# Taking 81 matmuls whose results nobody reads out of TensorE's instruction stream, at fifteen places

## What is computed

```python
x = x + L0_xattn(ln(x), ctx)   # 16 heads, causal mask: only the first 64 context rows of a batch count
x = x + L0_attn(ln(x))         # keys and values through a latent of width 64
x = x + L0_ffn(ln(x))          # bf16, 32 experts, top 4 by sigmoid gate, and a shared expert
x = x + L1_xattn(ln(x), ctx)   # one shared key/value head of width 16, all 1601 context rows
x = x + L1_attn(ln(x))         # causal attention, its own residual and layernorm with gamma, beta inside
x = x + L1_ffn(ln(x))          # 8 experts, each token goes to the one with the largest gate
```

## Time and profile before

| | |
|---|---|
| time, three runs | 552.41 us median (551.35 to 553.02) |
| the profiled execution | 552.53 us, span 550.6 us |
| busy share of the span | PE 94%, PE weight loads 66%, DVE 59%, ACT 55%, POOL 23% |
| matmuls | 6427, of which 81 by L1305 |
| mean granted TensorE clock | 0.996 |

### The profile page before, as it was taken

How to read it: one execution, slowest core, us unless ns; L and a number is a source line. 1 busy time by engine, 2 the same in 40 slices (tenths; PEclk the granted TensorE clock), 3 DMA queues, 4 the chain that set the end, 5 groups by cost and what they waited for, 6 DMA issues and landing times.

```text
span 550.6 us, 15198 instructions
## 1 busy us (share of the span) xinstructions
PE 519.7 (94%) x6427; PEld 363.7 (66%) x6427; DVE 325.7 (59%) x672; ACT 300.3 (55%) x511; POOL 124.2 (23%) x217
## 2 busy tenths in 40 slices
PE   3999999889999999889999999999979999999997
PEld 2666567546665666435776767676556657999996
DVE  4455475276666665768999999998146685011011
ACT  0356566676656565358887777877714412432221
POOL 5203602644333333340000000000060043000004
PEclk9999999999999999999999999999999998999999
DMA  8914620805554453820000000000080001798823
GB/s 325 402 45 162 228 92 9 284 8 149 146 158 138 147 155 99 301 83 2 4 3 4 4 2 4 3 4 4 2 307 1 1 2 39 240 353 271 309 90 95
DMA packets 35074, 64.37 MB, mean 117 GB/s; under 512 B 3296, under 2 KB 24800, under 8 KB 34624
## 3 DMA queue, kind: packets, MB, share of 16 engines
q1 hardware_dynamic: 34480, 62.35, 34.3%
q0 software_dynamic: 384, 1.05, 0.6%
q10 hardware_dynamic: 144, 0.01, 0.0%
HBM read 59.40 MB, written 4.00 MB: 115 GB/s over the span
## 4 chain that ended last, share of the span: by engine, by line
PE 84%; DVE 8%; POOL 2%; DMA 2%; ACT 2%; issue 2%; SPq 0%; POOLq 0%; DVEq 0%; ACTq 0%
PE ps L1342 14%; PE ps L1612 10%; PE ps L1743 9%; PE ps L1711 8%; PE ps L1757 7%; PE ps L1626 7%; PE ps L1935 6%; PE ps L1443 4%; PE ps L1317 2%; PE ps L1456 2%; PE ps L1469 2%; PE ps L1423 2%; DVE region L1119 1%; DMA ctx64T<-in_ctx64T 1%; PE ps L1367 1%
## 5 line engine op out<-in xcount | busy, mean ns | idle before, releaser
L1119 DVE TENSOR_REDUCE region<-ps 128x1 f32<-128x512 f32 x192 | 124.1, 687 | 17.9 <-PE ps L1711 17.9
L807 ACT ACTIVATE region<-ps 128x1024 f32<-128x1024 f32 (+1 forms) x112 | 105.9, 963 | 19.7 <-PE ps L1743 19.2
L1711 PE MATMUL ps<-ctx_kT,region 96*32 96x512 bf16 x768 | 82.0, 383 | 2.5 <-DVE region L1119 1.8
L1743 PE MATMUL ps<-region,ctx_kT 98*32 98x512 bf16 x832 | 72.5, 381 | 0.6 <-ACT region L785 0.4
L1757 PE MATMUL ps<-region,ctx_v 128*32 128x128 f32 (+1 forms) x1664 | 70.2, 272 | 0.0
L1612 PE MATMUL ps<-region 128*128 128x512 f16 x264 | 62.9, 379 | 0.3 <-DMA region<-in_moe 0.3
L1757 PEld LDWEIGHTS ps<-region,ctx_v 128*32 128x32 f32 (+1 forms) x1664 | 56.7, 109 | 9.4 <-issue 0.3
L857 ACT ACTIVATE region<-ps,ctx_v 128x128 f32<-128x128 f32 x88 | 25.2, 369 | 60.8 <-PE ps L1342 60.8
L502 POOL TENSOR_TENSOR region<-region 128x512 f32<-128x512 f32 x33 | 38.2, 1157 | 64.7 <-ACT region L734 63.3
L1626 PE MATMUL ps<-region 128*128 128x256 bf16 x384 | 47.2, 273 | 0.9 <-DVE region L1066 0.9
L1626 PEld LDWEIGHTS ps<-region 128*128 128x128 bf16 x384 | 37.4, 98 | 12.3 <-DVE region L1066 1.5
(11 more groups left out here) (230 smaller groups left out, 839.9 us busy)
## 6 DMA issues: line engine op xcount, KB each, us to landing
region<-in_w SPq DMA_DIRECT2D x15, 1024.0 KB, 8.5
region<-in_ctxT SPq DMA_DIRECT2D x8, 1601.0 KB, 7.9
region<-gates SPq DMA_DIRECT2D x30, 256.0 KB, 3.4
ctx_kT<-in_w SPq DMA_DIRECT2D x7, 1024.0 KB, 7.3
region<-in_moe SPq DMA_DIRECT2D x33, 192.0 KB, 2.4
attn_weights<-in_wall SPq DMA_DIRECT2D x1, 2152.0 KB, 21.9
slots_x<-zeros SPq DMA_DIRECT2D x1, 1408.0 KB, 10.5
ctx_v<-in_b2row SPq DMA_DIRECT2D x1, 1024.0 KB, 4.6
```

What stands on the lines that cost most here:

```text
L807: act.activation(probs[u % NP_][:, 0:512 * n_keys], ps[:, pr:pr + n_keys, :].rearrange("p b n -> p (b n)"), ACT.Exp).then_inc(mq["exp"], 1)
L1119: ins = dve.tensor_reduce(mp[g % 2][:, j // 3, j % 3:j % 3 + 1], bank(4 + n % 2), AX.X, ALU.max)
L1711: ins = pe.matmul(ps[32 * i:32 * i + 32, at, :], QT[0:KQ, b, h + i // 2, 32 * (i % 2):32 * (i % 2) + 32], kT[0:KQ, b, 512 * c:512 * c + 51 ...
L1743: ins = pe.matmul(ps[32 * c:32 * c + 32, 2 * (u % 2) + i, :], kT[0:KQ2, b, k * P + 32 * c:k * P + 32 * c + 32], QT[0:KQ2, b, 8 * r:8 * r + ...
```

## The change

The helper and its fifteen calls are deleted; every other instruction stays in its place.

```diff
-            def keep_clock(n, at):
-                for _ in range(n):
-                    pe.matmul(bank(at), ident_b, mask_b, start=True, stop=True, skip_group_check=True)
-
...
             up(1, (0,))
-            keep_clock(2, 6)
             keys_turn(7, 0)
...
             wq, wo = w("1x", 0, D), w("1x", D + 32, D)
-            keep_clock(14, 5)
             pe.wait_ge(mq["ln"], 1)
...
             pe.wait_ge(mq["qf"], TT)
-            keep_clock(7, 7)
             rows(0)
-            keep_clock(2, 7)
             scores(0)
...
             project_out(TT - 1)
-            keep_clock(10, 1)
             pe.wait_ge(mq["exp"], NH * HS)
...
             unit_turn(23)
-            keep_clock(2, 4)
             unit_values(22)
-            keep_clock(2, 4)
             unit_values(23)
-            keep_clock(3, 4)
             y_turn("1a", 1)
-            keep_clock(3, 7)
             take_head("O", "1a", 1)
...
             norm_turn("m1", 0)
-            keep_clock(2, 7)
             logits(0)
-            keep_clock(20, 7)
             norm_turn("m1", 1)
-            keep_clock(2, 7)
             logits(1)
-            keep_clock(2, 7)
             pe.wait_ge(m1["mask"], 1)
             positions(0)
             positions(1)
-            keep_clock(2, 7)
             pe.wait_ge(m1["mask"], 2)
...
             positions(3).then_inc(m1["pos_ps"], 1)
-            keep_clock(8, 7)
```

## The result

| | before | after |
|---|---|---|
| time | 552.71 us (551.35 to 556.61, 4 runs) | 561.40 us (561.26 to 562.37, 4 runs) |
| ratio to before | | 1.0149, 95% interval 1.0097 to 1.0202 |
| profiled execution, span | 552.53 us, 550.6 us | 562.37 us, 560.5 us |
| mean granted TensorE clock | 0.996 | 0.952 (0.954 to 0.966 in the other three) |
| matmuls recorded | 6427 | 6338 |

By the ratio the change costs 8.2 us (1.49%, interval 5.4 to 11.2 us); 8.25 us were forecast. The two medians lie 8.7 us apart. The kernel after does less work: TensorE's busy time fell from 519.7 to 511.9 us. (89 fewer matmuls are recorded; 81 were taken out, and of eight others the record is missing.) These are the busy line, the clock line and the chain line of the page of the kernel after. The clock line has one digit, in tenths of full speed, for each fortieth of the span.

What follows compares the result with a forecast made beforehand. TensorE, holding 84% of the chain of waits, was taken to bound the kernel. Clock-fall losses of 1.8 + 1.6 + 2.3 + 0.1 + 2.45 = 8.25 us on 552.53 gave 560.8 us, own range 558.2 to 564.3, stated range 555.5 to 564.8.

Steps and rivals of the forecast that it cites:

- What comes back outweighs what leaves: Whole kernel: about 1.8 us of TensorE work leaves the path, about 10 us come back as slow matmuls.
- The rate at half clock: After a fall: eight projections cost 1.78 us more, four 0.89, four transposes 0.4; weight loads double.
- The length of dense slow work, 3.3 to 5.8 us: After each fall, this much dense TensorE work runs at half speed, losing 1.7 to 2.9 us, taken 2.3.
- 221 us, 1.8: Fourteen removed: nothing gained, the clock falls, slow transposes and projections follow; 1.1 to 2.9 us lost, taken 1.8.
- 238 us, 1.6: Seven and two removed at 238 and 240 us: 0.3 gained, a fall costs 1.9; net 1.6 us.
- 402 us, 2.3: Ten removed: gain 0; norm_turn and 32 dense projections behind run slow, 1.7 to 2.9 us, taken 2.3.
- 439 us, +0.1: Ten removed from 439 to 444 us: 0.2 gained, DVE hides most of the slow projection; net -0.2 to +0.4.
- 447 and 458 us, 2.45: Way into m1: DVE's inputs 1.5 us later, nearly eating 1.35 gained before `dispatch`; slow `dispatch` and `up(0)` cost 2.3.
- The one occasion: Before the fall at 457.8 us: 2.43 us busy in 3.30 already cost the clock, so emptier stretches would too.
- Two places only: Rival: the clock falls only at 221 us and the way into m1; +3.75, 556.3 us; chance 0.20.
- The other side: Rival: the clock holds and the removed matmuls' time is won, mainly at 458 us; -1.85, 550.7 us; chance 0.06.
- The lasting low clock: Rival: bursts from 225 to 241 us don't raise the clock; queries, maxima and loop start slow; +12, about 565 us; chance 0.06.

Runs made afterwards that it cites:

- the place alone: Only the fourteen matmuls at 221 us left out of the kernel before; ratio 1.0005 (0.9982 to 1.0027), +0.3 us.
- 2.96 alone: Local loss in the trace with only the ten matmuls at 402 us left out of the kernel before; timed ratio 1.0017 (0.9990 to 1.0045).
- The two other traces: The kernel before run twice more, unchanged, for a second and third trace; measured 551.68 and 551.46 us.
- the second trace: The first of two further runs of the kernel before, unchanged; measured 551.68 us.

## Why the prediction was right, and where it was not

- **What comes back outweighs what leaves.** Right. Of 1.85 us that were to leave the path, 1.2 (458 us) and 0.2 (238 us) did.
- **The rate at half clock.** Right: 2.08 for four projections, 3.75 for eight, 1.88 for `logits(1)` (about 2 expected), 1.09 for four transposes. The transposes lengthened too: four of L1367 take 0.63 to 0.66 us at a granted clock of 1.00 and 1.09 to 1.12 at 0.50. So the rule of the Trainium skill, TensorE: Matmul & The Clock Gate, section on PE-mode transpose, that the high clock does not engage for transposes, does not hold here, if these transposes run in the mode that it speaks of.
- **The length of dense slow work, 3.3 to 5.8 us.** Too narrow. At 240 us the clock was low from before 241.9 to 250.6, 8.7 us of nearly dense work; at 412 us it was 3.2 us. The two ends of the range came from one occasion each.
- **221 us, 1.8.** Right in the trace (1.64), down to the parts: projections 0.9, transposes 0.4. Not found in the timed runs of the place alone.
- **238 us, 1.6.** The fall came, its size was off: 3.30. The failed term is "of 3.3 to 5.8 us low from 241.35 on": it was 8.7. The loop gave up 3.3 of them, near the rates forecast (0.85 in the first 1.9, then a third).
- **402 us, 2.3.** 1.55 in the trace of after, 2.96 alone. The chain there is dense on TensorE as read, so half of each low microsecond was lost; the clock happened to rise early. But with the ten in place 0.3 to 1.5 us are lost there in nine of ten traces, so "the whole loss counts" put too much on the change: timed it is +0.9 us (-0.5 to +2.5).
- **439 us, +0.1.** Too low: 0.48 and 0.85. The step that failed is that "DVE is busy with the layernorm of the first half" until the projection is there, so that only tile 3 comes late. Already tile 2 did: in the timeline of DVE after, below, its addition L1199 waits 0.37 us for TensorE, and starts 5.85 us later than before (446.39), L905 ahead of it only 5.40.

```profile
451.14 0.73 DVE L905 TENSOR_SCALAR xn<-x,ln_mean_var,ln_rstd 128x256 f32<-128x256 f32 x2 [1.14 <-POOL ln_rstd L449]
452.24 0.42 DVE L1199 TENSOR_TENSOR region<-ps,x_plus_bias 128x256 f32<-128x256 f32 x1 [0.37 <-PE ps L1338]
```

- **447 and 458 us, 2.45.** Right (2.68): transposes 0.45, `logits(1)` 0.83, `dispatch` started within 0.1 us of its old distance from the last norm_turn and lost 2.6.
- **A premise failed without moving the sum much.** I took the first trace's clock as that of before. The two other traces of it are low at 238 and 402 us and not at 458. With them as the base the forecast would be some 0.7 us lower (less 1.4 and 0.4, plus 1.15). The one occasion from which I read what an emptier engine does to the clock does not repeat either: in the second trace TensorE did as little from 454.4 to 457.7 us (2.38 of 3.30 us, before 2.43), and the clock stayed at 1.00. With it the 1.2 us at 458 us were not there to be won: `dispatch` starts 1.22 us earlier in that trace with the eight in place.
- **Luck.** That 8.25 met 8.2 so closely is luck. In the profiled pair 238 us was 1.7 too low and 402 us 0.75 too high, the places sum to 9.64, and the interval of the timed cost is 5.4 to 11.2 us. What is shown is the direction, the mechanism and the rough size.
- **Rivals.** Two places only: excluded for the kernel after, in whose trace the clock fell at every place named. The figure of the Trainium skill, TensorE: Matmul & The Clock Gate, on the warm-up budget (below 1%) is given there for the ramp of a typical kernel. It was no bound for this one, which has several: the added low stretches cost 1.49% (0.97 to 2.02). The other side: its 1.2 us were there, and `dispatch` took back 2.6. The lasting low clock: not at 225 to 230 us, where it rose at 230.2, but it describes 240 to 250 us better than my forecast did.

## What to carry to other kernels

Matmuls that nobody reads cost almost nothing where TensorE waits anyway, and the clock can pay for them: look not at their count but at what TensorE would do in the holes around them. Before such work is taken out, or put in, read the mean granted clock over many executions, since one trace shows one of several patterns. Even what stands directly ahead of the critical step can pay: at half clock the eight held `dispatch` back by 1.2 us, but with them in place the clock was full there in six of seven traces, and then `dispatch` started as early as without them. Leaving them out cost 1.3 us (0.2 to 2.4).

## What the runs showed that I had not expected

- The same program has different low stretches from execution to execution: at 458 us in the first trace of before, at 238 and 402 us in the two others, and mean clocks of 0.984 to 0.997 in 81 runs.
- The clock can fall among the very matmuls meant to fill a hole: in the second trace of before TensorE was busy for 2.98 of 3.20 us at 0.50 from 401.8 to 405.0 us.
- The first rise comes at different times too (11.7 us in the trace of after, with a low stretch again from 15.2 to 18.6, and near 20.7 in the first of before), worth 1.7 us at the start.
- Half the clock does not mean half the speed of the kernel: 39 us more at 0.50 cost 8.2 us.
